# A graph attention kernel: a larger descriptor ring, smaller last sub blocks, and single rows fetched by SyncE

## What is computed

```python
for l in range(3):
    f_out = leaky_relu((nf @ W_ni)[src] + (nf @ W_nj)[dst] + ef @ W_fij + bias, 0.2)
    e = einsum('ehd,hd->eh', f_out.reshape(E, H, D), attn)      # 4 scores an edge
    a = exp(e - segment_max(e, dst)[dst])
    a = a / segment_sum(a, dst)[dst]
    h = (nf @ W_node).reshape(N, H, D)
    nf = segment_sum(h[src] * a[:, :, None], dst).mean(axis=1)
    ef = f_out.reshape(E, H, D).mean(axis=1)
return x + nf
```

## Time and profile before

| what | us |
|---|---|
| median of 3 runs | 3349.8 (3348.49 to 3351.11) |
| the profiled execution | 3350.28 |
| its span, first to last instruction | 3348.5 |
| busy: PE, POOL, DVE, ACT | 2666.5, 2450.9, 2181.6, 1647.9 |

### The profile page before, as it was taken

The page is one execution under the profiler, slowest core; times in us unless marked ns, Lnnn a source line. Parts: engine busy times, 40 slices in busy tenths (PEclk is TensorE's granted clock), DMA queues, the critical chain, the costliest instruction groups (busy, mean ns, idle before and its releaser), DMA issues.

```text
span 3348.5 us, 34593 instructions
## 1 busy us (share of the span) xinstructions
PE 2666.5 (80%) x8951; PEld 1981.0 (59%) x8960; DVE 2181.6 (65%) x5339; ACT 1647.9 (49%) x3374; POOL 2450.9 (73%) x2589
## 2 busy tenths in 40 slices
PE   2299988878888278888898888826988888888894
PEld 1177766656665256666666666524666666666663
DVE  5288876767667247676676666734766767667664
ACT  0166655555555145555555555513554545555552
POOL 5777777777776777777777777767777777777773
PEclk8655555555556555555555555755555555555555
DMA  6143434343332323333333333232223332233222
GB/s 228 50 125 107 137 108 123 95 123 95 109 101 95 110 74 109 95 123 95 124 108 95 123 95 101 89 110 83 86 86 105 99 105 86 86 105 99 82 67 94
DMA packets 131420, 345.96 MB, mean 103 GB/s; under 512 B 48155, under 2 KB 89007, under 8 KB 111651
## 3 DMA queue, kind: packets, MB, share of 16 engines
q1 hardware_dynamic: 45892, 282.18, 22.4%
q0 software_dynamic: 82496, 46.67, 9.4%
q10 hardware_dynamic: 2838, 14.91, 1.1%
HBM read 130.86 MB, written 212.74 MB: 103 GB/s over the span
## 4 chain that ended last, share of the span: by engine, by line
POOL 55%; issue 19%; PE 17%; DMA 6%; DVE 3%; ACT 1%; POOLq 0%; DVEq 0%; ACTq 0%
POOL rows L462 53%; PE f_ps L576 6%; PE f_ps L585 5%; DMA rows<-nf_tab,src_sb 4%; PE xT_ps L566 4%; POOL edge_first L473 2%; DMA U<-fix_tab 1%; DVE U L1095 1%; PE f_ps L595 1%; PE wide_ps L660 1%; PE xT_ps L647 0%; POOL z L516 0%; DMA nf_tab<-nf 0%; PE f_ps L660 0%; ACT up L755 0%
## 5 line engine op out<-in xcount | busy, mean ns | idle before, releaser
L462 POOL DMA_INDIRECT rows<-nf_tab,src_sb x2418 | 2282.7, 944 | 759.9 <-issue 727.8
L585 PEld LDWEIGHTS f_ps<-w_out,lr 128*128 128x128 f32 x4836 | 1149.5, 327 | 609.7 <-issue 575.1
L576 PE MATMUL f_ps<-xT,w_edge 97*128 97x512 f32 x1212 | 1135.7, 1038 | 9.3 <-ACT xT L700 9.3
L566 PE MATMUL xT_ps<-ident,rows 128*97 128x128 f32 x2418 | 682.5, 435 | 510.6 <-DMA rows<-nf_tab,src_sb 352.4
L585 PE MATMUL f_ps<-w_out,lr 128*128 128x36 f32 (+1 forms) x4836 | 1032.7, 367 | 12.9 <-DVE lr L1029 12.7
L1029 DVE TENSOR_TENSOR lr<-f_ps,f_low 128x512 f32<-128x512 f32 x606 | 415.4, 685 | 873.3 <-ACT f_low L709 868.8
L566 PEld LDWEIGHTS xT_ps<-ident,rows 128*97 128x97 f32 x2418 | 508.8, 275 | 548.0 <-DMA rows<-nf_tab,src_sb 350.8
L1095 DVE TENSOR_TENSOR_SCAN U<-wide_ps,U 128x272 f32<-128x272 f32 (+1 forms) x1224 | 795.6, 713 | 2.3 <-ACT wide_ps L744 1.8
L700 ACT ACTIVATE xT<-xT_ps 97x512 f32<-97x512 f32 x606 | 357.2, 589 | 409.1 <-PE xT_ps L566 407.6
L709 ACT ACTIVATE f_low<-f_ps 128x512 f32<-128x512 f32 x606 | 360.2, 594 | 335.1 <-PE f_ps L576 334.0
L744 ACT ACTIVATE wide_ps<-e_dec 128x289 f32<-128x289 f32 (+1 forms) x612 | 403.3, 675 | 159.9 <-DVE U L1095 158.0
(11 more groups left out here) (141 smaller groups left out, 618.2 us busy)
## 6 DMA issues: line engine op xcount, KB each, us to landing
u_tab<-up SPq DMA_DIRECT2D x150, 1088.0 KB, 4.2
rows<-nf_tab,src_sb POOLq DMA_INDIRECT x2418, 2.4
first_st<-edge_first SPq DMA_DIRECT2D x48, 768.0 KB, 6.0
ef_tab<-ef_new SPq DMA_DIRECT2D x32, 768.0 KB, 4.2
ef_st<-ef_tab SPq DMA_DIRECT2D x32, 768.0 KB
edge_first<-first_st ACTq DMA_DIRECT2D x16, 768.0 KB
ef_st<-in_edge_attr_dram SPq DMA_DIRECT2D x16, 672.0 KB
U<-fix_tab SPq DMA_DIRECT2D x3, 1062.5 KB
```

Source lines behind the costliest of these rows:

```text
L462: eng.indirect_dma_start(rows[q % RING][:, c * K:c * K + D], None, nf_tab[:, :], bass.IndirectOffsetOnAxis(ap=src_sb[:, t:t + 1], axis=0)) ...
L566: mm = eng.transpose(xT_ps[y][0:K, u * P:(u + 1) * P], rows3[q % RING][:, a * GT + u, :], ident[:, :])
L576: eng.matmul(f_ps[n % 3][:, 0:grp_w(g) * P], w_edge[l][:, :], xT[y][0:K, 0:grp_w(g) * P], start=True, stop=True).then_inc(f_ready, 1)
L585: mm = eng.matmul(f_ps[n % 3][:, u * m:(u + 1) * m], lr[y][:, u * P:(u + 1) * P], w_out[l][:, 0:m], start=True, stop=True)
```

## The change

The changed kernel differs in these ways:

- `dynamic_dma_scratch_size` is 32768 bytes of each partition; without the argument it is 16384. To make room, `s_nd` and the two `first_st` buffers share their bytes, and `holds` moves to `ef_new`.
- The last column (47) of super blocks 1, 3, ... 15 is no longer gathered by POOL. SP fetches its 128 rows with one DMA each, whose address is a register; 16 addresses are loaded into registers at a time from a new tile `one_idx`. For each of these super blocks the 128 are spread in pieces of 16 or 32 over 6 sub blocks ahead of it, behind `store_u`; for super block 1 the first 80 stand at the start of the layer, behind the first two `load_first`. PE's `turn` of the group waits for a semaphore more.
- `one_idx` is loaded in the prologue behind the store of `nf_tab`, and DVE multiplies it by 32.
- The last 10 groups make 5 sub blocks of 2 groups (NB = 53). The tight order begins at `END` = NG - 14, and the last 8 groups (`TIGHT` = NG - 8) are taken one by one: a group's scores come before the next group's transposes. `KEEP_WARM` is 4; in the last 8 groups 2 useless matmuls stand behind the transposes and 4 behind `edges`.
- `LEAD0` is 20.
- POOL issues 4 columns of `z`, not 8, ahead of the scatter `fix_tab`.
- ACT waits for the landed `nf_tab` before its stores of zeros.
- The last `store_ef` of a layer stands behind the last `store_u`.

```diff
-LEAD0 = 16
+LEAD0 = 20
+ZEARLY = 4
+REGS = 16
-KEEP_WARM = 3
+KEEP_WARM = 4
+FILL_TURN = 2
+FILL_EDGES = 4
+    SUB = ([range(g, g + GB) for g in range(0, NG - 10, GB)]
+           + [range(g, g + 2) for g in range(NG - 10, NG, 2)])
+    NB = len(SUB)
+        s_nd = sb("s_nd", [P, NCOL * HD])
+        first_st = [s_nd[:, s * SUP * D:(s + 1) * SUP * D] for s in range(2)]
-        END = NG - 10
+        END = NG - 14
+        TIGHT = NG - 8
+        def ones_after(b):
+            for v in range(NS):
+                if sp_sup(v):
+                    i = b - (SUBS * v - 7)
+                    if 0 <= i < 6:
+                        return v, P * i // 6 // REGS * REGS, P * (i + 1) // 6 // REGS * REGS
+            return 0, 0, 0
...
+                def fetch_ones(q, p0, p1):
+                    if p0 == 0 and q >= RING:
+                        eng.wait_ge(prod_done, subs_to(q - RING))
+                    c = SUP - 1
+                    for p in range(p0, p1, REGS):
+                        _, at = nc.values_load_multi_w_load_instructions(
+                            one_idx[q % NS:q % NS + 1, p:p + REGS], engines=[SP_ENGINE],
...
+                        for u, row in enumerate(at):
+                            eng.dma_start(rows[q % RING][p + u:p + u + 1, c * K:c * K + D],
+                                          nf_flat[:, bass.ds(row, D)]
+                                          ).then_inc(one_rows[q % RING], 16)
...
                     load_first(q0 + 1)
+                    if l == 0:
+                        eng.wait_ge(one_made, 1)
+                    eng.wait_ge(tab_out, (l + 1) * 16)
+                    for b in range(-7, 0):
+                        v, p0, p1 = ones_after(b)
+                        fetch_ones(q0 + v, p0, p1)
...
                             store_u(k0 + b)
+                            v, p0, p1 = ones_after(b)
+                            fetch_ones(q0 + v, p0, p1)
...
+                        if by_sp(t):
+                            continue
...
-                    gather_z(0)
+                    gather_z(0, part_cols[0][:ZEARLY])
...
+                        if gathered(g) < grp_w(g):
+                            eng.wait_ge(one_rows[q % RING], ones_to(q))
...
+                    turn(TIGHT)
+                    scores(TIGHT - 1)
+                    edges(TIGHT)
+                    scores(TIGHT)
+                    for g in range(TIGHT + 1, NG - 2):
+                        turn(g)
+                        warm(g + 1, FILL_TURN)
+                        edges(g)
+                        warm(g + 1, FILL_EDGES)
+                        scores(g)
...
                 eng.wait_ge(first_zero, 1)
+                eng.wait_ge(tab_out, 16)
...
+                    for b, g in ((NB - 4, NG - 6), (NB - 3, NG - 4)):
+                        soften(b)
+                        product(b)
+                        leaky(g)
+                        add_up(b, 0)
+                        add_up(b, 1)
+                        add_up(b, 2)
+                        add_up(b, 3)
+                        leaky(g + 1)
...
-    nc = _bacc.Bacc("TRN2", target_bir_lowering=False, num_devices=1)
+    nc = _bacc.Bacc("TRN2", target_bir_lowering=False, num_devices=1,
+                    dynamic_dma_scratch_size=32768)
```

More of the change, by code:

```diff
@@ L61, in sub_w, with sub_at, sub_of, subs_to @@
     def sub_w(b):
-        return min(SB, T - b * SB)
+        return min(SUB[b].stop * GT, T) - sub_at(b)
+    def sub_at(b):
+        return SUB[b].start * GT
+    def sub_of(g):
+        return next(b for b in range(NB) if g in SUB[b])
+    def subs_to(q):
+        l, s = divmod(q, NS)
+        return l * NB + sum(sub_at(b) < (s + 1) * SUP for b in range(NB))
     def grp_w(g):
@@ L103, in egat_kernel @@
         rows3 = [r[:, :].rearrange("p (t k) -> p t k", k=K) for r in rows]
-        first_st = [sb(f"first_st{s}", [P, SUP * D]) for s in range(2)]
+        s_nd = sb("s_nd", [P, NCOL * HD])
+        first_st = [s_nd[:, s * SUP * D:(s + 1) * SUP * D] for s in range(2)]
         first3 = [a[:, :].rearrange("p (t d) -> p t d", d=D) for a in first_st]
@@ L125, in egat_kernel @@
         src_sb = sb("src_sb", [P, T], I32)
+        one_idx = sb("one_idx", [NS, P], I32)
         same = sb("same", [P, T])
@@ L218, in egat_kernel @@
         src_rows = [[sem(f"src_rows{s}_{a}") for a in range(GS)] for s in range(RING)]
+        one_in = sem("one_in")
+        one_made = sem("one_made")
+        one_rows = [sem(f"one_rows{s}") for s in range(RING)]
         ef_in = [sem(f"ef_in{s}") for s in range(2)]
@@ L285, in ef_in_count, with sp_sup, by_sp, gathered @@
             return 16 * sum(ef_loads(a) for a in range(q % 2, q + 1, 2))
+        NONE = NS - 1
+        REST1 = max((REST - SUP) // SUP + 1, 0)
+        def sp_sup(v):
+            return v % 2 == 1 and v < NONE
+        def by_sp(t):
+            return t % SUP == SUP - 1 and sp_sup(t // SUP)
+        def gathered(g):
+            return sum(not by_sp(g * GT + u) for u in range(grp_w(g)))
         def rows_sem_to(q, a):
-            return 16 * sum(grp_w((v % NS) * GS + a) for v in range(q % RING, q + 1, RING)
+            return 16 * sum(gathered((v % NS) * GS + a) for v in range(q % RING, q + 1, RING)
                             if (v % NS) * GS + a < NG)
+        def ones_to(q):
+            return 16 * P * sum(sp_sup(v % NS) for v in range(q % RING, q + 1, RING))
+        def ones_after(b):
[5 more added lines that the diff above has]
+            return 0, 0, 0
         def carry_of(u, w):
@@ L414, in _ @@
                     if l < L - 1:
+                        store_ef(q0 + NS - 1)
                         load_ef(q0 + NS)
@@ L606, in _ @@
                     warm(END, WARM_UP)
-                    for g in range(END, NG - 1):
+                    for g in range(END, TIGHT):
                         turn(g)
@@ L610, in _ @@
                         edges(g)
-                        if g < NG - 2:
-                            warm(g + 1, KEEP_WARM)
+                        warm(g + 1, KEEP_WARM)
+                    turn(TIGHT)
[8 more added lines that the diff above has]
+                        scores(g)
+                    turn(NG - 2)
+                    warm(NG - 1, FILL_TURN)
+                    edges(NG - 2)
                     turn(NG - 1)
@@ new lines, in _ @@
+                    k = k + 2
+                    take_xT(NG - 10)
+                    take_scores(NG - 11)
+                    lower(NG - 10)
+                    weigh(k)
+                    widen(k, 0)
+                    widen(k, 1)
+                    lay_out(k - 1)
+                    take_xT(NG - 9)
+                    take_scores(NG - 10)
+                    lower(NG - 9)
+                    widen(k, 2)
+                    widen(k, 3)
+                    k = k + 1
+                    take_xT(TIGHT)
@@ new lines, in _ @@
+                    take_scores(TIGHT - 1)
+                    lower(TIGHT)
+                    weigh(k)
+                    widen(k, 0)
+                    widen(k, 1)
+                    lay_out(k - 1)
+                    widen(k, 2)
+                    take_scores(TIGHT)
+                    take_xT(TIGHT + 1)
+                    widen(k, 3)
+                    lower(TIGHT + 1)
+                    lay_out(k)
+                    take_scores(TIGHT + 1)
+                    for g in (NG - 6, NG - 4):
+                        k = k + 1
+                        take_xT(g)
+                        weigh(k)
+                        widen(k, 0)
+                        lower(g)
+                        widen(k, 1)
+                        widen(k, 2)
+                        take_scores(g)
+                        take_xT(g + 1)
+                        widen(k, 3)
+                        lower(g + 1)
+                        lay_out(k)
+                        take_scores(g + 1)
@@ L838, in _ @@
                 eng.memset(dcol, N).then_inc(zeroed, 1)
+                eng.memset(one_idx[:, :], 0)
                 eng.memset(src_sb[:, :], 0).then_inc(zeroed, 1)
@@ L943, in _ @@
                 eng.memset(rows3[2][:, :, D:C], 1.0)
+                eng.wait_ge(one_in, 32)
+                eng.tensor_scalar(one_idx[:, :], one_idx[:, :], float(D), None, ALU.mult
+                                  ).then_inc(one_made, 1)
                 eng.wait_ge(run_in, 16)
@@ L1144, in _ @@
                     add_up(NB - 2, 1)
+                    soften(NB - 1)
                     add_up(NB - 2, 2)
-                    soften(NB - 1)
                     add_up(NB - 2, 3)
```

111 lines of the change are left out of this document (68 added, 43 removed).

## The result

The changed kernel takes 3327.1 us (median of 6 runs, 3321.1 to 3329.4) against 3349.6 (6 runs, 3346.9 to 3355.9): a ratio of 0.9929, interval 0.9919 to 0.9939. That is 22.5 us less, where 61.6 were forecast, and just above the range. The profiled execution took 3321.1 us, the fastest of its six, with a span of 3319.3.

A forecast was written before the change was run, and what follows sets the result against it. POOL's gathers, 1.2486 us each, were taken to pace a layer, with PE near at 88%. Gains of 30.0 + 9.7 + 3.4 + 16 + 2.5 = 61.6 us gave 3288.2 us, range 3270 to 3325.

The forecast's parts named there:

- Fewer gathers: POOL's gathers in each layer: 8 columns a layer leave POOL, 24 x 1.2486 = 30.0 us won.
- LEAD0: POOL's wait at 146.26 in the first layer: a lead of 20 takes it away, 3.4 us won.
- SP's pace: SP's row DMAs: 0.45 us a row, 58 of 118.6 us, hidden in SP's waits; limit 0.85 us a row.
- the second rival: SP can't keep up with its rows: sets in at 0.85 us a row, up to 1150 us lost; chance 0.10.
- The layer ends: POOL's idle time at the three layer ends shrinks through shorter DVE work: 4.5, 4.5 and 7, together 16 us won.
- the moved `store_ef`: Last `store_ef` of a layer moved: lies in SP's and DVE's waits, 0 us.
- The rival of the low clock: PE's clock stays low at layer ends: 1.7 us behind per group; 3312 us for half the time, 3336 throughout; chance 0.14.
- ZEARLY: Scatter `fix_tab` goes out 5.0 us sooner after each layer's end: 0 in layers 0 and 1, 2.5 us won in layer 2.
- The start: Prologue: ACT waits for the node table's store, which lands in 3.8 us, so POOL begins at 18.3; 9.7 us won.
- The ring: Larger ring for POOL's gathers: none waited for room before, so 0 us.

The follow-up runs named there:

- every_fourth: Changed kernel with SP fetching the last column of every fourth super block (12 columns), not every second; 3329.0 us, 0.9960 of the kernel before.
- overlap_fourth: Changed kernel with last 8 groups overlapped, SP's rows for every fourth super block only, and the former order between layers; 3314.6 us, 0.9914 of the kernel before.

## Why the prediction failed

- **Fewer gathers, `LEAD0`, SP's pace: right.** 20.1 us in layers 1 and 2 where 20.0 were forecast; in layer 0 12.3 for 13.4 (the first two gathers took 1.80 and 1.14 us). 0.41 to 0.45 us a row, where 0.45 was taken, holds for the chips of the first kind only. That the runs first shown met such a chip was luck: on the others the second rival, put at 0.10, came true.
- **The layer ends: the failed step, forecast -16, measured +6.3.** "I take 4.5 in layers 0 and 1" and "7" in layer 2 priced the tail alone and took the lag ahead of it as unchanged, without a reason. The tails gave 15.9 us; that the sum met 16 so closely is partly luck, since the moved `store_ef`, put at 0, is in it, and layer 2 gave 4.9 instead of 7. The lag at the last turns grew by 22.3 us in sum. Overlapped, the last 8 groups had made up 5.6 and 3.1 us in layers 0 and 1 and lost 1.0 in layer 2; one by one they lose 3.4, 7.7 and 4.3. The text had the number for this, 4.8 us a group "just inside POOL's 5.0", and used it only for a rival about the clock: it should have asked with what lag PE enters these groups and whether it can leave them with less. That the order is the cause is shown by `every_fourth` and `overlap_fourth`: lags of 7.0 and 6.9 us at the first of these groups, 12.4 and 2.8 at the last turn.
- **The rival of the low clock, put at 0.14: true in part.** It had PE fall 1.7 us behind in each group at the low clock. In layer 1, with four groups at 0.50 to 0.67, PE fell back 1.2 to 2.8 us in each, and the three layers lost 16.5 us up to their largest lag, most of it at a low clock. But in layer 0 a group took 6.6 us at full clock, and at full clock nothing is made up. How much would be lost with a full clock throughout wasn't tried. The rival's own sum is off besides: (13.6 + 6) x 3 = 59 us for a clock low throughout and 29 for half the time, not 48 and 24.
- **`ZEARLY`: sign wrong between the layers, +5.8 for 0.** The forecast took the scatter as ready 5 us sooner and did not ask when DVE's result is there; `overlap_fourth`, with `ZEARLY` = 8, has the 3 us a layer back. It moves `store_ef` as well, and no run on the first kind moves only one of the two; the waits of 2.51 and 2.42 us at the scatter speak for `ZEARLY`. In layer 2 1.4 of 2.5 us came.
- **The start: mis-sized,** 7.5 for 9.7: 6.15 us from the store to the first gather, not 3.8. Why is open.
- **The ring: 0,** as forecast, shown only on a chip of the second kind.
- **Left over.** The ledger's 29.2 us are of two single executions; the medians lie 22.5 apart, and the changed kernel's runs spread over 8.3 us. Where its slower runs lose was not seen.
- **Open.** Which part of the lag is the low clock's, and which the dummy matmuls' at that clock. The overlapped order with all 24 columns never met a chip of the first kind. From 0.9958 and 30 us it would be near 0.987: argued, not measured. `overlap_fourth`, 0.9914, is the fastest measured; its interval overlaps that of the changed kernel.

## What to carry over

Where a stage hands over from one engine to a chain of others, write down the lag with which the chain enters and its pace against the feeder's; an order that shortens the last link but runs at the feeder's pace keeps every microsecond of lag to the end, and adds to it where the clock is low. Ask of each wait that is moved forward whether what it waits for is there yet. And a hiding place with a thin margin (0.45 us used of 0.85 a row) is a hiding place on one chip: run it on several.
